# Perceiver block on one core: tile 1's last context piece, tile 2's entry norm and the order of steps 1 and 2

## The reference

```
x = x + fake_quant(layernorm(x)) @ fake_quant(ctx)          # cross attention, quantized to 0..255
h = layernorm(x)
q, k, v = split(h @ Wqkv)                                   # 32 heads of 32, one key head and one value head
p = softmax(where(causal, q @ k.T * scale + alibi, -1e30))
x = x + (p @ v) @ Wo
h = layernorm(x)
r = softmax(h @ gate_w.T)                                   # 8 experts
x = x + ((h * (r @ in_scale)) @ sign(W).T) * (r @ out_scale) + bias
```

## Time and profile before

| | |
|---|---|
| median of 3 runs | 413.5 us (412.54 to 413.9) |
| the profiled execution's own time | 411.08 us |
| its span in the trace | 409.3 us |
| PE busy | 359.6 us |
| DVE, ACT, POOL busy | 311.4, 255.6, 132.8 us |
| HBM read | 85.05 MB |
| mean granted clock of TensorE | 0.979 of full speed |

### The profile page before, as it was taken

One profiled execution on the slowest core, in us unless ns is written; L12 is line 12 of the kernel. 1 busy time (PEld: TensorE's weight loads), 2 busy tenths in 40 slices (PEclk: granted clock), 3 DMA queues, 4 the chain that ended last, 5 costly groups with the idle time before them and its releaser, 6 DMA issues.

```text
span 409.3 us, 9998 instructions
## 1 busy us (share of the span) xinstructions
PE 359.6 (88%) x4145; PEld 232.8 (57%) x4145; DVE 311.4 (76%) x591; ACT 255.6 (62%) x307; POOL 132.8 (32%) x148
## 2 busy tenths in 40 slices
PE   0426954899889899999999999999999999999996
PEld 0113932784444784579556865696559755874444
DVE  6888798898838689769976998589858975496353
ACT  3757977867787768773886488647866632334121
POOL 5310024305430324512451146123712371027041
PEclk9968996999999999999999999999999999999999
DMA  7999999379999579865867586748576000100002
GB/s 297 412 363 410 409 406 382 109 239 339 361 406 388 198 218 408 309 227 166 289 238 233 147 303 226 239 126 315 200 254 151 16 2 0 55 2 0 2 1 104
DMA packets 30243, 91.56 MB, mean 224 GB/s; under 512 B 8112, under 2 KB 8496, under 8 KB 30192
## 3 DMA queue, kind: packets, MB, share of 16 engines
q1 hardware_dynamic: 28320, 84.42, 57.9%
q10 hardware_dynamic: 1872, 6.40, 4.1%
HBM read 85.05 MB, written 4.19 MB: 218 GB/s over the span
## 4 chain that ended last, share of the span: by engine, by line
PE 57%; DMA 15%; DVE 13%; ACT 6%; SPq 4%; issue 4%; POOL 0%; DVEq 0%; POOLq 0%
DMA ring<-ctx 15%; PE R L1598 9%; PE T L1423 6%; PE R L1368 5%; PE R L1370 5%; PE R L1369 5%; PE C L1404 5%; PE R L1459 4%; PE R L1462 3%; PE R L1461 3%; ACT b L583 3%; PE T L1504 3%; PE R L1488 2%; SPq L370 2%; SPq L407 1%
## 5 line engine op out<-in xcount | busy, mean ns | idle before, releaser
L583 ACT ACTIVATE b<-ring,quant,qpar 128x2048 uint8<-128x2048 f32 x62 | 128.9, 2094 | 19.3 <-DMA ring<-ctx 12.1
L1459 PE MATMUL R<-T_hi,Wqkv_hi 128*128 128x128 f16 x448 | 77.9, 220 | 0.0
L1461 PE MATMUL R<-T_lo,Wqkv_hi 128*128 128x128 f16 x448 | 77.7, 219 | 0.0
L1462 PE MATMUL R<-T_hi,Wqkv_lo 128*128 128x128 f16 x448 | 77.7, 219 | 0.0
L1404 PE MATMUL C<-b,aT 128*64 128x512 f16 x256 | 36.6, 422 | 16.4 <-ACT b L583 11.4
L485 POOL TENSOR_TENSOR Pr<-Pr,mx 128x512 f32<-128x512 f32 x32 | 35.4, 1117 | 32.7 <-DVE mx L1067 32.7
L333 POOL TENSOR_TENSOR Pr<-Pr,mx 128x512 f32<-128x512 f32 x20 | 20.7, 1042 | 76.7 <-DVE mx L1061 76.7
L1459 PEld LDWEIGHTS R<-T_hi,Wqkv_hi 128*128 128x128 f16 x448 | 43.9, 98 | 2.0
L1461 PEld LDWEIGHTS R<-T_lo,Wqkv_hi 128*128 128x128 f16 x448 | 43.9, 98 | 0.1
L1462 PEld LDWEIGHTS R<-T_hi,Wqkv_lo 128*128 128x128 f16 x448 | 43.8, 98 | 0.0
L1368 PE MATMUL R<-Wo,attT_hi 128*128 128x512 f16 x112 | 42.5, 379 | 0.6 <-DVE attT_lo L1079 0.5
(11 more groups left out here) (172 smaller groups left out, 838.5 us busy)
## 6 DMA issues: line engine op xcount, KB each, us to landing
ring<-ctx SPq DMA_DIRECT2D x64, 1024.0 KB, 8.1
ring<-L_attn_Wo SPq DMA_DIRECT2D x4, 1024.0 KB, 8.6
ring<-L_ffn_weight SPq DMA_DIRECT2D x4, 1024.0 KB, 6.0
Wo<-L_attn_Wqkv SPq DMA_DIRECT2D x7, 544.0 KB, 15.1
X<-x ACTq DMA_DIRECT2D x6, 512.0 KB, 3.8
out<-X ACTq DMA_DIRECT2D x6, 512.0 KB, 6.1
X<-x SPq DMA_DIRECT2D x2, 512.0 KB, 11.4
sgn<-L_attn_Wqkv SPq DMA_DIRECT2D x1, 544.0 KB, 17.8
```

The costliest lines, as they stand in the source:

```text
L583: e.activation(b8[:, c % BRING, :], ring[:, slot, :], ACT.Identity, scale=qR2, bias=qZ2).then_inc(s_rf[slot], 1)
L1459: e.matmul(dst, hi, rows[0], start=k == 0 and g == 0, stop=False, skip_group_check=True)
L1461: e.matmul(dst, hi, rows[1], start=False, stop=False, skip_group_check=True)
L1462: last = e.matmul(dst, lo, rows[0], start=False, stop=k == KT - 1, skip_group_check=True)
```

## The change

- SP: the load of X[2], which stood ahead of pieces 6 and 7 of tile 1's context, comes behind all of tile 1. Pieces 0 to 3 of tile 2 are issued ahead of the bias and of the transpose of tile 2's rows, where it was pieces 0 and 1.
- conv(1, 7) moves from ScalarE to VectorE, and TensorE's last context piece waits for both conversions.
- The statistics, norm0_rows and norm0_quant of tile 2 move back in VectorE's list: the statistics to the place ahead of k_lo, the others behind tile 1's softmax, norm0_quant behind the remainders of tile 1's PT00 and PT01.
- o_hi of a tile's first half waits for s_wolow, a new semaphore that counts when the second column half of the projection has read the low chunks, instead of for the whole projection.
- TensorE: ten filler matmuls ahead of tile 1's last context piece, 12 and 5 for the 6 and 4 about the transposes of the second norm; project(s, 0, high) and project(s, 1, high) each move ahead of a part of tile 1's attention.
- ScalarE, VectorE and GpSimd: other orders in step_1, as the diff shows. 

```diff
@@ -261,6 +261,7 @@
         s_rcp = sem("s_rcp")
         s_nrm = sem("s_nrm")
         s_ohi = sem("s_ohi")
+        s_wolow = sem("s_wolow")
         s_wo = sem("s_wo")
         s_x2 = sem("s_x2sum")
         s_xl2 = sem("s_xl2")
@@ -390,9 +391,6 @@
                 if t == 0:
                     e.dma_start(X[1][:, :], x_v[1]).then_inc(s_x[1], 16)
                 load_context(t, 4, 2)
-                if t == 1:
-                    e.wait_ge(s_prep, 3)
-                    e.dma_start(X[2][:, :], x_v[2]).then_inc(s_x[0], 16)
                 if t == 3:
                     turn_over(t)
                 if t == 0:
@@ -406,15 +404,17 @@
             for k in range(KT):
                 e.dma_start(wqkv_raw[k], wqkv_v[:, k, :]).then_inc(s_lw[k], 16)
             loads(1)
+            e.wait_ge(s_prep, 3)
+            e.dma_start(X[2][:, :], x_v[2]).then_inc(s_x[0], 16)
             for k in range(KT // 2):
                 load_piece(k, weight_uses("wo"), weight_piece(k), wo_v[:, 2 * k:2 * k + 2, :])
             for k in range(KT // 2):
                 load_piece(k, weight_uses("ffn"), weight_piece(k), wt_v[:, 2 * k:2 * k + 2, :])
-            load_context(2, 0, 2)
-            turn_over(2)
+            load_context(2, 0, 4)
             e.dma_start(bias_sb[:, :], bias.rearrange("(o n) -> o n", o=1).broadcast_to([P, H]))\
                 .then_inc(s_bias, 16)
-            load_context(2, 2, ITEMS - 2)
+            turn_over(2)
+            load_context(2, 4, ITEMS - 4)
             for t in range(3, TILES):
                 loads(t)
 
@@ -496,7 +496,6 @@
                 subtract_max(e, 0, 0, 1)
 
             def step_1(s, ahead):
-                inv_std(0, 2)
                 subtract_max(e, 0, 1, 0)
                 subtract_max(e, 0, 1, 1)
                 normalize(0, 0, 0)
@@ -504,17 +503,18 @@
                 inv_std(1, 1)
                 normalize(0, 1, 0)
                 normalize(0, 1, 1)
+                inv_std(0, 2)
                 subtract_max(e, 1, 0, 0)
                 subtract_max(e, 1, 0, 1)
+                subtract_max(e, 1, 1, 0)
+                subtract_max(e, 1, 1, 1)
                 normalize(1, 0, 0)
                 normalize(1, 0, 1)
-                subtract_max(e, 1, 1, 0)
-                subtract_max(e, 1, 1, 1)
                 normalize(1, 1, 0)
                 normalize(1, 1, 1)
                 inv_std(2, 0)
+                with_bias(0)
                 with_row_sum(2)
-                with_bias(0)
                 inv_std(0, 3)
                 inv_std(2, 1)
                 inv_std(1, 2)
@@ -628,7 +628,10 @@
             def o_hi(s, h):
                 m = s.i - 1
                 e.wait_ge(s_pv, m * 4 + 2 * h + 2)
-                at_least(e, s_wo, m * 2)
+                if h == 0:
+                    at_least(e, s_wolow, m)
+                else:
+                    at_least(e, s_wo, m * 2)
                 e.activation(attT_half(0, h), T[:, s.bank(f"O{h}"), :]
                              .rearrange("p (b g t) -> p b g t", b=2, t=S),
                              ACT.Identity, scale=C_ATT).then_inc(s_ohi, 1)
@@ -744,13 +747,12 @@
 
             def step_1(s, ahead):
                 exp(0, 0, 0)
+                exp(0, 0, 1)
                 conv(1, 6)
-                exp(0, 0, 1)
-                conv(1, 7)
                 exp(0, 1, 0)
+                exp(0, 1, 1)
                 pt_hi(s, 0, 0)
                 pt_hi(s, 0, 1)
-                exp(0, 1, 1)
                 wo_hi(0)
                 t1_hi(s, 0)
                 t1_hi(s, 1)
@@ -773,25 +775,25 @@
                 exp(1, 0, 0)
                 exp(1, 0, 1)
                 sign(3)
+                exp(1, 1, 0)
+                exp(1, 1, 1)
                 pt_hi(ahead, 0, 0)
                 pt_hi(ahead, 0, 1)
                 conv(2, 0)
-                exp(1, 1, 0)
-                exp(1, 1, 1)
                 o_hi(ahead, 0)
-                conv(2, 1)
                 pt_hi(ahead, 1, 0)
                 pt_hi(ahead, 1, 1)
+                conv(2, 1)
                 conv(2, 2)
+                o_hi(ahead, 1)
                 conv(2, 3)
-                o_hi(ahead, 1)
                 conv(2, 4)
                 t2_copy(s, 0)
                 t2_copy(s, 1)
+                router_exp(s)
                 conv(2, 5)
-                router_exp(s)
+                rt_copy(s)
                 conv(2, 6)
-                rt_copy(s)
                 conv(2, 7)
                 xs_hi(s, 0)
                 xs_hi(s, 1)
@@ -972,7 +974,7 @@
 
             def norm0_rows(t):
 
-                at_least(e, s_T1, {0: 0, 1: 0, 2: 2}.get(t, 2 * t))
+                at_least(e, s_T1, 2 * t if t > 1 else 0)
                 e.wait_ge(s_rstd[0], t + 1)
                 link(e.tensor_scalar(tok[:, :], x_in(t)[:, :], mv[0][:, 0:1], rstd[0][:, 1:2],
                                      ALU.subtract, ALU.mult))
@@ -1207,11 +1209,10 @@
                 softmax_in(0, 0)
 
             def step_1(s, ahead):
-                stats0(2)
                 softmax_in(0, 1)
                 row_sum(0, 0, 0)
+                conv(1, 7)
                 row_sum(0, 0, 1)
-                norm0_rows(2)
                 x1(s)
                 pt_lo(s, 0, 0)
                 norm1(s)
@@ -1223,24 +1224,26 @@
                 wo_lo(0)
                 v_lo(s)
                 o_lo(s, 0)
+                stats0(2)
                 k_lo(s)
                 wo_lo(1)
-                wo_lo(2)
                 pt_lo(s, 1, 0)
                 pt_lo(s, 1, 1)
+                wo_lo(2)
                 q_lo(s, 0)
                 wo_lo(3)
                 softmax_in(1, 0)
                 o_lo(s, 1)
                 q_lo(s, 1)
-                norm0_quant(2)
+                softmax_in(1, 1)
                 row_sum(1, 0, 0)
                 row_sum(1, 0, 1)
-                softmax_in(1, 1)
+                norm0_rows(2)
+                row_sum(1, 1, 0)
+                row_sum(1, 1, 1)
                 pt_lo(ahead, 0, 0)
                 pt_lo(ahead, 0, 1)
-                row_sum(1, 1, 0)
-                row_sum(1, 1, 1)
+                norm0_quant(2)
                 o_lo(ahead, 0)
                 x2(s, 0)
                 x2(s, 1)
@@ -1251,11 +1254,11 @@
                 stats0(3)
                 router_max(s)
                 router_probs(s)
+                x2(ahead, 0)
                 xs(s, 0)
                 xs(s, 1)
                 xs_lo(s, 0)
                 xs_lo(s, 1)
-                x2(ahead, 0)
                 x2(ahead, 1)
                 x1(ahead)
                 norm1(ahead)
@@ -1395,7 +1398,7 @@
                     at_least(e, s_v, t)
                 c = 2 * pair + 1
                 e.wait_ge(s_rf[c % RING], uses(t, c) + 1)
-                if (t, c) in ((0, 7), (1, 3)):
+                if (t, c) in ((0, 7), (1, 3), (1, 7)):
                     e.wait_ge(s_rf[(c - 1) % RING], uses(t, c - 1) + 1)
 
                 def products(k, lhs, first, last):
@@ -1526,6 +1529,8 @@
                                          k == 0, k == KT - 1)
                 if k == KT - 1:
                     last.then_inc(s_wo, 1)
+                elif n == 1 and k == KT // 2 - 1:
+                    last.then_inc(s_wolow, 1)
 
             def t2(s):
                 m = s.i - 1
@@ -1654,12 +1659,14 @@
 
             def step_1(s, ahead):
                 context(1, 2)
+                e.wait_ge(s_stt, piece(0, 0, 1) + 1)
+                keep_clock(10, bank=1)
                 context(1, 3)
                 pt(s, 0, 0)
                 pt(s, 0, 1)
-                keep_clock(6)
+                keep_clock(12)
                 t1(s)
-                keep_clock(4)
+                keep_clock(5)
                 kv(s)
                 query(s, 0, low[:2])
                 pv(s, 0)
@@ -1676,11 +1683,11 @@
                 project(s, 0, low)
                 scores(s, 1)
                 project(s, 1, low)
+                project(s, 0, high)
                 pt(ahead, 0, 0)
                 pt(ahead, 0, 1)
-                project(s, 0, high)
+                project(s, 1, high)
                 pv(ahead, 0)
-                project(s, 1, high)
                 pt(ahead, 1, 0)
                 pt(ahead, 1, 1)
                 project(ahead, 0, low)
```

## The result

The changed kernel takes 407.39 us (median of 4 runs, 407.37 to 407.67). The kernel before took 413.02 us beside it (4 runs, 409.11 to 413.9). The ratio is 0.9875, with a 95% interval of 0.983 to 0.992: 5.6 us less. I had written 411.0 us with a range of 409.2 to 413.2, so the direction was right and the size was not: 2.5 us forecast, 5.6 measured. The profiled execution of after has a span of 405.6 us and took 407.38 us; against the profiled 411.08 us of before that is 3.7 us. The other 1.9 us lie between the profiled execution of before and its median. Repeated unchanged on two chips, the difference of the medians was 5.7 and 5.3 us.

The account below looks back on a forecast made before the run. Step 1 was taken as bound by context loads and ScalarE's conversions, later steps by matmuls. A 2.7 us gain less small lock wait and late landing gave 2.5 us, 408.6 profiled, 411.0 us median; range 409.2 to 413.2.

Parts of the forecast that it names:

- The head's mechanism: Tile 1's last context pieces: earlier transfer, conversion on VectorE and held clock start its transposes at 68.9, gain 2.75 us.
- the lock: VectorE's piece 7 conversion waits for the port shared with GpSimd: 0.15 us taken, 1.0 at the other end.
- The stations of the middle and the second half: Tile 1's exponentials near 95, PT11 at 104.0, T2 copies at 114.3, tile 2's transposes at 131.9.
- I count ScalarE full: Second half: ScalarE sets the pace without waiting for transfers; the argument against the 4.0 us gain.
- the transfer rival: Second half: transfers were the real bound, ScalarE's small waits close; gain 4.0 us, 409.5 us, chance 0.12.
- The moved norm: Tile 2's norm behind tile 1's second softmax on VectorE: whole cost 0.7 us of waiting before PT11.
- the last one: Final scaling: profiled 411.08 less 2.5 gives 408.6; the median 0.6% above the profile makes it 411.0 us.
- The slower rival: Tile 2's piece 4 lands at 118 behind the transpose's slow issue; 417.0 us, chance 0.10.
- the row of an idle queue: Tile 2's transpose by transfer on an idle queue: 1.23 us to issue and 3.8 to land.

Follow-up runs that it names:

- The kernel before without the jump: Kernel before, without the jump over the uneven zero point part of context(2, 0) and the 24 matmuls it leads over: 409.55 us (0.9877 to 0.9933).
- without the late orders: Kernel after with before's late orders on TensorE (projections behind PT and PV) and ScalarE (from the fourth sign on): 409.9 us, 1.7 more than after.
- the one part out of both kernels: Kernels before and after, each without the uneven zero point part of tile 2's first context pair and its jump: 409.55 and 408.56 us.
- the one with the new loads: Kernel before with only SP's tile 2 loads reordered (pieces 0 to 3, bias, transpose, pieces 4 to 7): 414.17 us (0.9971 to 1.0026).
- The two with 22 fillers: Two profiled measurements of the kernel before with 22 filler matmuls ahead of tile 1's last context piece: 410.7 and 410.51 us.
- the first repeat: Kernel before, unchanged, measured and profiled again: median 413.42 us over 12 runs, 407.45 to 415.01.

## Why the prediction was wrong in size

**The head's mechanism was right, its size partly by luck.** Tile 1's transposes were forecast at 68.9 and came at 69.00, with the clock held and the piece in 1.05 us. But this execution's entry ran 0.5 us earlier. Counted from the context piece before (58.38 and 57.87), the gain is 2.25 us, not the 2.75 of the forecast. Inside it, the lock cost 0.46 us (1.81 for 1.35) where I took 0.15: the transfer landed at about 61.0, and GpSimd was in its multiply from 60.75 to 61.79, not at the end of its second subtraction. The conversion on ScalarE would have ended only 0.26 us later, so nothing hung on it. Most of the head's worth is the clock: undoing the fillers loses some 2.9 us of the median. In the profile 1.7 of them are there at tile 2: 1.1 in the head, and 0.6 where the clock fell a second time.

**The stations of the middle and the second half were right, their ground was not.** Forecast and found: tile 1's exponentials at 95 and 94.88, PT11 at 104.0 and 104.39, the T2 copies at 114.3 and 113.98, tile 2's transposes at 131.9 and 131.06. But the step "I count ScalarE full", with which I set the transfer rival aside, failed: in the profile that I read, four conversions waited 1.75 us for context, and those waits closed. That rival priced the gain at 4.0 us; between the profiled executions it was 3.7, against the 2.5 that I forecast. The kernel before without the jump tells how much was a disturbance: with the old orders and nearly no such wait, its stretch is 60.93 us, 1.9 less than in the profile before. After's is 62.06. So between these two profiles the second half *loses* 1.1 us, against the 2.4 us that the head gains (71.39 to 69.00). The moved norm is the likely cost, but no run has it alone; without the late orders the loss would be 1.7 more. The change itself is then worth about 1.3 us (132.32 to 131.06 in the profiles, 409.55 to some 408.2 in the medians), and not 2.5. With the one part out of both kernels it is 1.0 us, 409.55 and 408.56 on two chips, and the intervals (0.9877 to 0.9933, 0.9849 to 0.9915) overlap: that the change itself gains anything is likely, not shown.

**The step that failed most is the last one:** "The profiled execution took 411.08 us ... The median of the runs is 413.5, 0.6% above it, so 411.0 us". I scaled the difference between profile and median as if both kernels had it. After doesn't: its profiled execution took 407.38 us and its median is 407.39. Of the 3.6 us that the forecast missed, 2.4 are this step, the other 1.2 lie between the profiled executions, where I had put the waits for context at nothing. What before has is a stop: three of the four profiles of the unchanged kernel, and the one with the new loads, show TensorE standing 3.36 to 3.63 us ahead of the router's last matmul; the fourth, mine, had the late context instead. The two with 22 fillers don't have it, and none of the ten profiles of after and its variants has it. Moving the block's end away from the router, by leaving one part out, removes the stop from the profile, takes 3.7 us off the median and brings the spread down to 1.2 us. That is shown. What one execution with the stop costs is less even: the first repeat with it took 411.85 us, 0.8 more than my profile without, the others 412.33 to 414.63, where the clock fell behind the stop. The measured 5.6 us are then these 3.7 us or so and between 1.0 and 1.9 of the change's own. That the change took the stop away was no part of the prediction: it is luck.

The Trainium skill has this rule (Runtime: NRT & Kernel Launch, Instruction fetch mechanics): code is fetched ahead in order, and a jump whose target isn't loaded waits for a fetch. By the rule a stop stands at the jump. The traces don't bear that out here: the stop comes 67 matmuls behind the jump, in straight code, at the end of a block, and the others stand at block ends too. I had not looked for waits for code at all: they would have been a rival with a price only from their own measurement, 3.63 us.

**The slower rival** (piece 4 late) did not come: the transpose by transfer took 1.33 us to issue, as the row of an idle queue said.

**What stays open.** Why the eighth block of code comes at 106 to 111 us in after and at 117 in three of the four profiles of before (in after it had landed 2.9 us or more before its first matmul): the queues may hold less context while SP stands at the transpose until 103.3, which was not tried by itself, and the new loads alone leave the stop. Why fillers and the missing part don't add up in the kernel before. Why the block due near 280 us is late in some executions (stops of 0.25 to 1.9 us) and not in others, two of after's four profiles among them. And why the version with the fillers, which has no stop at the router in two profiles, still spreads over 5.2 us: the stop isn't the whole of before's spread.

## What to carry to other kernels

Profile the kernel before more than once when its runs spread by more than the change is worth: behind 4 to 8 us of spread was, for a good part, a 3.6 us stop that the one profile at hand did not contain, and a change can be worth more by stepping around such a stop than by what it was worked out for. Look for idle time that ends by "issue" in the middle of a run of equal matmuls, and for a packet of the queue of kind "instruction" that starts some 2.5 us before its end: here that was a wait for the next block of code. Code that never runs counts too, since it moves where the blocks end. And before an experiment with empty instructions is believed, see that the compiled program contains them. Fillers that hold the clock through one wait only put its fall off if the next wait is left uncovered: with 22 of them at the first wait, the clock fell at the second in two of three profiles. Ten and twelve at both held it there in eight of nine profiles (in the ninth, with the conversion on ScalarE, it fell at 64.2 us); two of the eight had it fall later, at 98.4 and 104.9.

## What the runs showed of the hardware

TensorE's code came in packets of 16,384 bytes, 256 instructions, 39 in an execution. Where one came late, TensorE stood at the end of its block until 1.2 to 1.6 us after the packet had ended: 3.63 us at the worst place, with transfers running at 409 GB/s beside it (115 to 120 us), 0.2 to 1.9 us at others (near 117, 153, 238 and 280 us), and at most of the other block ends nothing. A transpose by transfer took between 1.33 and 5.55 us to issue, growing with the context queued ahead: 5.55 behind four pieces, 2.5 to 3.9 behind two, 1.33 when SP had issued nothing for 7.4 us (95.9 to 103.3). VectorE's 128x2048 conversion took 1.81 us when its piece landed in GpSimd's 1.04 us multiply, and 1.56 to 2.21 us in eight other profiles with such a multiply beside it, against 1.35 alone.
